# Attention in a language-model tower: the two heads of a pair in turns, both divided before one output projection, all sums of probabilities on GpSimd

## The reference, cut to what matters

```python
h = tok_table[x] + bias                                   # x: (2, 2048) tokens, 256 wide
def attn(x):                                              # x = layernorm(h)
    xn = layernorm(x) * norm_g + norm_b
    q = heads(xn @ Wq); k, v = split(x @ Wkv)             # 16 heads of 64
    k, v = concat(null_k, k), concat(null_v, v)           # 2 null keys: 2050 keys
    q, k = l2norm(q) * q_scale, l2norm(k) * k_scale
    sim = 8 * q @ k.T - slope[head] * abs(j - i)          # causal
    return merge(softmax(sim) @ v) @ Wout
h = h + attn(layernorm(h))
h = h + moe(layernorm(h))                                 # 8 experts of 256, top 2, and a shared one
```

## Time and profile before

| | |
|---|---|
| runs shown | 3328.92 us median of 3 (3328.67 to 3331.39) |
| profiled execution, its own time | 3325.87 us |
| its span, first to last instruction | 3323.9 us |
| PE, PEld, DVE, ACT, POOL busy | 90%, 44%, 61%, 45%, 49% |
| mean granted clock of PE | 0.962 of full speed |
| chain that ended last, shares | PE 63%, DVE 15%, POOL 11%, issue 9%, ACT 2% |

### The profile page before, as it was taken

The page is one execution under the profiler, slowest core; times in us unless marked ns, Lnnn a source line. Parts: engine busy times, 40 slices in busy tenths (PEclk is TensorE's granted clock), DMA queues, the critical chain, the costliest instruction groups (busy, mean ns, idle before and its releaser), DMA issues.

```text
span 3323.9 us, 50152 instructions
## 1 busy us (share of the span) xinstructions
PE 2989.6 (90%) x14241; PEld 1454.6 (44%) x14241; DVE 2013.1 (61%) x5648; ACT 1490.9 (45%) x2988; POOL 1631.9 (49%) x2152
## 2 busy tenths in 40 slices
PE   3589898989898987898989898989898989999999
PEld 2333434343434343434443434343434344666666
DVE  6666675666566658575757575756566663444444
ACT  3344555555555554555555555555555543111111
POOL 6454656565676564556565656565656543000000
PEclk9799999999999998999999999999999999999999
DMA  1000000000010000000000000000000100000000
GB/s 41 14 14 9 14 9 15 8 17 6 18 30 18 5 18 4 11 12 12 11 12 11 12 11 14 10 15 8 17 6 12 51 13 1 1 1 19 7 0 26
DMA packets 97495, 44.27 MB, mean 13 GB/s; under 512 B 38224, under 2 KB 96208, under 8 KB 97232
## 3 DMA queue, kind: packets, MB, share of 16 engines
q1 hardware_dynamic: 95696, 36.88, 4.3%
q0 software_dynamic: 1536, 4.20, 0.4%
HBM read 19.65 MB, written 4.19 MB: 7 GB/s over the span
## 4 chain that ended last, share of the span: by engine, by line
PE 63%; DVE 15%; POOL 11%; issue 9%; ACT 2%; DMA 0%; SPq 0%; DVEq 0%; POOLq 0%; ACTq 0%
PE ps L1146 13%; PE ps L1191 7%; PE ps L1204 7%; DVE ps L880 6%; PE ps L1130 5%; PE ps L1075 5%; PE ps L1163 5%; PE ps L1103 5%; PE ps L1131 4%; PE ps L1072 4%; PE ps L1153 3%; POOL rnorm L592 2%; POOL acc L628 2%; POOL tab_l L606 2%; DVE acc L915 1%
## 5 line engine op out<-in xcount | busy, mean ns | idle before, releaser
L715 ACT ACTIVATE probs<-ps,btab 128x512 f32<-128x512 f32 (+4 forms) x1408 | 768.3, 591 | 625.2 <-PE ps L1131 331.4
L628 POOL TENSOR_TENSOR acc<-acc,probs 128x512 f32<-128x512 f32 (+4 forms) x896 | 860.1, 960 | 162.6 <-ACT probs L715 84.3
L1146 PE MATMUL ps<-probs,arena 128*64 128x512 f32 (+4 forms) x2816 | 742.3, 530 | 0.0
L880 DVE CUSTOM_DVE_ANT_0 ps<-ps,tab_l 128x512 f32<-128x512 f32 (+1 forms) x896 | 568.2, 676 | 283.6 <-PE ps L1103 283.2
L1130 PE MATMUL ps<-arena 128*128 128x512 f16 (+4 forms) x1408 | 476.8, 339 | 0.7 <-issue 0.6
L1131 PE MATMUL ps<-arena 65*128 65x512 f16 (+9 forms) x1408 | 470.7, 336 | 0.0
L1163 PE MATMUL ps<-wo,otf 128*128 128x256 f32 (+1 forms) x1024 | 358.3, 432 | 5.6 <-DVE h L931 4.6
L931 DVE SCALAR_TENSOR_TENSOR h<-ps,rl,h 128x256 f32<-128x256 f32 x512 | 245.1, 479 | 132.0 <-PE ps L1163 131.5
L1103 PE MATMUL ps<-arena 64*128 64x512 f16 (+4 forms) x1408 | 256.7, 344 | 74.4 <-DVE mx L880 67.0
L592 POOL TENSOR_TENSOR rnorm<-nsq,minus_half 128x4 f32<-128x4 f32 (+1 forms) x272 | 298.3, 1097 | 22.7
L1072 PE MATMUL ps<-wqkv,xnT 128*128 128x128 f32 x1024 | 183.3, 304 | 136.0 <-DVE h L931 110.8
(11 more groups left out here) (128 smaller groups left out, 3753.7 us busy)
## 6 DMA issues: line engine op xcount, KB each, us to landing
arena<-arena SPq DMA_DIRECT2D x512, 32.0 KB, 1.9
wqkv<-in_Wkv SPq DMA_DIRECT2D x32, 128.0 KB, 2.4
wo<-in_Wout SPq DMA_DIRECT2D x64, 64.0 KB, 2.2
arena<-in_w SPq DMA_DIRECT2D x2, 2048.0 KB, 10.4
out<-h SPq DMA_DIRECT2D x8, 512.0 KB, 2.9
wqkv<-in_Wq SPq DMA_DIRECT2D x16, 128.0 KB, 2.4
arena<-augs SPq DMA_DIRECT2D x128, 1.0 KB
l_col<-arena SPq DMA_DIRECT2D x128, 2.0 KB, 2.0
```

The costliest lines, as they stand in the source:

```text
L628: pool.tensor_tensor(a, a, probs[0:rows, n % PB, 0:GW - c0], ALU.add).then_inc(sum_pool, 1)
L715: nc.scalar.activation(probs[0:rows, n % PB, 0:w], bank(S0 + n % 2)[0:rows, 0:w], ACT.Exp, bias=btab[0:rows, hh, z:z + 1]).then_inc(exp_do ...
L880: nc.vector.tensor_tensor_reduce(bank(A0 + hd)[:, 0:w], bank(A0 + hd)[:, 0:w], tab, 1.0, NEG, ALU.add, ALU.max, mx[:, hd, it, c:c + 1]).th ...
L1146: mm(bank(O0 + o % 2)[DH * z:DH * z + DH, c0:GW], vt[t % 2][0:rows, jt, hd, :], probs[0:rows, n % PB, 0:GW - c0], start=(jt <= (1 if ig el ...
```

## The change

The order and the work of the attention part change together:

- The blocks of the two heads come in turns (`block_of`): block m is head m % 2 of block m // 2. Head 0 writes rows 0 to 63 of the output bank and head 1 rows 64 to 127, in all groups.
- `sums` makes two matmuls with 64 output rows each, one per head, so that one bank holds the sums of both heads, each repeated over the rows of its head. A new DVE step, `divide`, takes the reciprocal of this 128x512 bank and multiplies the output bank by it. `wout` then is 4 matmuls per group for both heads, and `add_o` a plain addition. `keep_o`, `keep_l`, `turn_l` and `inv_l` go; Wout is held once, in one DMA per pair.
- `sum_p`: POOL adds up all groups (`DVE_SUMS` is empty). In groups 1 to 3 the first block isn't copied: the second block's addition reads both from `probs`. `acc` has 3 buffers instead of 2.
- `raw` goes: ACT copies q and k straight into `tqk`. `unit` is one multiplication for q and one per head for k, which takes the scale in as well; `scale_k` on POOL goes.
- `tables` moves from POOL to ACT; DVE adds the mask to `tab_r` before the first unit of a pair. The tables of pair t are planned at 88t-38, its projection from 88t-70 with a step of 5, its maxima from 88t-34.
- The start: fewer and later POOL steps for constants (`parameters` is separate), the zeros of the second arena later, shorter offsets between the steps of `embed` and `project`; the plan starts at -35 instead of -57, and the maxima of pair 0 are tied to the projections that they need. `embed` of the second sequence is spread with a step of 10 instead of 3.8 and ends in pair 7.

```diff
+    def block_of(m):
+        return (m % 2, *blocks[m // 2])
-    def side(m):
-        return m % 2 if blocks[m % BLKS][0] else 0
-    DVE_SUMS = (2,)
+    AB = 3
+    DVE_SUMS = ()
...
     def project(t, t0, step):
-            at(s0 + 2.9, "unit", t, s)
-            at(s0 + 3.0, "scale_k", t, s)
+            at(s0 + 2.6, "unit", t, s)
...
+        for ig in range(NG):
+            e0 = t0 + 2 * last_block[ig] + 1
+            at(e0 + 2.6, "sums", t, ig)
+            at(e0 + 3.2, "divide", t, ig)
+            for k in range(G):
+                w0 = max(e0 + 5.3, wout_from[0] + 2)
+                wout_from[0] = w0
+                at(w0, "wout", t, ig, k)
+                at(w0 + 0.6, "add_o", t, ig, k)
...
-    embed(0, -51, 2.2)
+    embed(0, -31, 2.6)
-    project(0, -44, 1.6)
-    maxima(0, -17, 0.9)
+    project(0, -24, 1.6)
+    maxima(0, -14.4, 1.1, lambda g: -24 + 1.6 * (2 * g + 1) + 8)
     for t in range(1, PAIRS):
-        project(t, PAIR * (t - 1) + 1.6, 3.2)
-        at(PAIR * t - 66.5 if t > 1 else 27, "tables", t)
-        if t > 1:
-            maxima(t, PAIR * t - 59.5, 1.85)
-        else:
-            maxima(t, 32, 1.75)
+        project(t, PAIR * t - 70, 5.0)
+        maxima(t, PAIR * t - 34, 1.85)
     for t in range(PAIRS):
+        at(PAIR * t - 38 if t else -16, "tables", t)
         attend(t, PAIR * t)
-        embed(b, PAIR * (b * NP - 2) + 50, 3.8)
+        embed(b, PAIR * (b * NP - 1) - 62, 10)
...
             def sum_p(t, m):
+                if on_dve or (ig > 0 and jt == 0):
                     return
+                if jt == (1 if ig else 0):
+                    need(pool, l_ready, (i - AB) // 2 + 1)
+                if ig == 0 and jt == 0:
+                    pool.tensor_copy(a, p).then_inc(sum_pool, 1)
                 else:
+                    first = ig > 0 and jt == 1
+                    pool.tensor_tensor(a, probs[0:rows, (n - 2) % PB, 0:GW] if first else a, p, ALU.add).then_inc(sum_pool, 1)
...
+            def tables(t):
+                need(act, a_read, 2 * UNITS * t)
+                need(act, aug_ready, NG * t)
+                for hd in range(2):
+                    nc.scalar.activation(tab_l[:, hd, :], pos[:, 0:512], ACT.Copy, scale=slope).then_inc(tab_ready, 1)
+                    nc.scalar.activation(tab_r[:, hd, :], pos[:, :], ACT.Identity, bias=back[:, hh:hh + 1], scale=slope).then_inc(tab_ready, 1)
+                    nc.scalar.activation(tab_k[:, hd, :, :], key0[:, :, :], ACT.Copy, scale=slope).then_inc(tab_ready, 1)
+                    nc.scalar.activation(tab_g[:, hd, :], group_pos[:, :], ACT.Copy, scale=slope).then_inc(tab_ready, 1)
...
             def unit(t, s):
+                if s < T:
+                    nc.vector.tensor_tensor(q, q, rnorm[0:rows, s % 2, 0:2].unsqueeze(2).to_broadcast([rows, 2, DH]), ALU.mult)
+                for hd in range(2):
+                    last = nc.vector.scalar_tensor_tensor(out=k[:, hd, :], in0=k[:, hd, :], scalar=rnorm[0:rows, s % 2, 2 + hd:3 + hd],
+                                                          in1=scl[0:rows, :], op0=ALU.mult, op1=ALU.mult)
...
+            def divide(t, ig):
+                o = NG * t + ig
+                dve.wait_ge(l_ready, o + 1)
+                nc.vector.reciprocal(rl[:, :], shared_of("sums", t, ig)[:, :]).then_inc(rl_ready, 1)
+                dve.wait_ge(rl_ready, o + 1)
+                dve.wait_ge(pv_done, PAIR * t + 2 * last_block[ig] + 2)
+                need(dve, w_ready, G * (o - 1))
+                nc.vector.tensor_tensor(otf[:, o % 2, :], bank(O0 + o % 2), rl[:, :], ALU.mult).then_inc(o_read, 1)
...
-                z = side(m)
-                mm(bank(O0 + o % 2)[DH * z:DH * z + DH, c0:GW], vt[t % 2][0:rows, jt, hd, :], probs[0:rows, n % PB, 0:GW - c0],
-                   start=(jt <= (1 if ig else 0)), stop=(jt >= G * ig + G - (1 if ig else 0))).then_inc(pv_done, 1)
+                mm(bank(O0 + o % 2)[DH * hd:DH * hd + DH, c0:GW], vt[t % 2][0:rows, jt, hd, :], probs[0:rows, n % PB, 0:GW - c0],
+                   start=(jt == 0), stop=(jt == G * ig + G)).then_inc(pv_done, 1)
...
+            def sums(t, ig):
+                for hd in range(2):
+                    last = mm(bank(z)[DH * hd:DH * hd + DH, :], ones[:, :], acc[:, (2 * (NG * t + ig) + hd) % AB, :], start=True, stop=True)
+            def wout(t, ig, k):
+                mm(bank(z)[:, 0:D], otf[:, o % 2, 128 * k:128 * k + 128], wo[:, r, :], start=True, stop=True).then_inc(w_ready, 1)
```

More of the change, by code:

```diff
@@ L923, in add_o @@
-            def add_o(t, hd, ig, k):
-                o = (2 * t + hd) * NG + ig
-                n = o * G + k
+                if jt == (1 if ig else 0):
+                    need(dve, l_ready, (i - AB) // 2 + 1)
+                if ig == 0 and jt == 0:
+                    nc.vector.tensor_copy(a, p).then_inc(sum_dve, 1)
+                else:
+                    first = ig > 0 and jt == 1
+                    nc.vector.tensor_tensor(a, probs[0:rows, (n - 2) % PB, 0:GW] if first else a, p, ALU.add).then_inc(sum_dve, 1)
@@ L1112, in scores @@
             def scores(t, m):
[L1113 removed]
+                hd, ig, jt, rows, c0 = block_of(m)
                 n, w = PAIR * t + m, GW - c0
```

295 lines of the change are left out of this document (120 added, 175 removed).

## The result

The changed kernel takes 3483.57 us (median of 4 runs, 3477.64 to 3484.27) against 3328.8 for the kernel before (4 runs, 3325.28 to 3331.39). The ratio is 1.0462, 95% interval 1.0444 to 1.048: 4.6% slower, where 9.6% faster was forecast. The profiled execution took 3477.64 us, its span is 3475.2.

What follows compares the result with a forecast made beforehand. PE was taken as the bound, with gaps mainly behind POOL's tables. Start -32, pair 0 -35, steady pairs -210, pair 6 -17 and pair 15 -25 sum to -319 from 3325.9: 3007, predicted 3010 us, range 2850 to 3140.

Steps and rivals of the forecast that it cites:

- The PE work: Steady pair: fewer or paired matmuls in `wout`, `sums` and group 0 of `values` save 17.5 us of 151.
- The reciprocal: New DVE division step: a reciprocal of 512 columns takes 3.4 us, or 4.3 by the skill's estimate.
- The stall behind it: PE waits after each division, in `scores_a` or `wout`: 2.2 us four times a pair, 8.8 us, ends 0 and 16.
- The tables on ACT: Eight table activations moved to ACT cost a steady pair 2 us, between 0 and 5.5.
- The gap behind POOL's tables: Projection wait for `add_o`, 7.9 us a pair, plus 1.4 of slow clock, goes when tables leave POOL: 9.3 us.
- DVE and POOL otherwise: Remaining load in a steady pair: DVE ends near 104 us, POOL at 102, costing PE 1 us.
- blocked `unit`: DVE's unit norm held up by POOL's SBUF use beyond the range; shares a 0.03 chance with a dearer reciprocal.
- POOL's jostling: POOL close to PE's pace in the wide blocks of a steady pair: 1 us a pair, ends 0 and 17.
- Rival 3: Slower kernel: POOL's waits per inverse norm push a steady pair over 171 us, whole up to 3500 us; chance 0.03.
- PE waits mostly for exponentials that wait for POOL: Stated sign of being wrong: POOL sets the pace in wide blocks, 3250 us, 3130 at half price; chance 0.22.
- Rivals 1: Division is covered, so a steady pair is PE-bound at 136.7 us and the whole takes 2840 us; chance 0.25.
- Rival 4: Two heads' matmuls don't overlap: two full blocks take 1.72 us, not 1.08; 18 us a pair, 3280 us; chance 0.02.

Runs made afterwards that it cites:

- The best version: Changed kernel with later unit norm, now on ACT, key scale on POOL, division in four, tables spread, projections 2 places earlier: 3027.4 us, ratio 0.9093.
- the single instruction: Changed kernel with the key scale left out, so the unit norm is one DVE multiplication instead of three narrow instructions: 3314.37 us.
- the improved one: Changed kernel with later unit norm, division in four parts and tables spread on ACT: 3141.36 us; with projections 2 places earlier 3064.83 us.

## Why the prediction was wrong

**The PE work** (17.5 us a pair off 151): right. The best version has 395.48 / 3 = 131.8 us of it at nearly the clock of before, where 133.5 was forecast. In the changed kernel it shows as 141, at a clock of 0.91: matmuls behind a gap run slower, as L1053 above. Apart from the 1.4 us behind the tables the sum had no term for that, and it is 7.5 of the 25.6 us by which a pair is over the forecast.

**The reciprocal**: right. 3.36 us for 64 of them, against 3.4; the 4.3 us, an estimate from the Trainium skill (VectorE: DVE Perf Modes, First, the fixed hardware budget), did not come. **The stall behind it**: right in place and about right in size. 8.8 us a pair was taken; cutting the division in four gave back 167 us, 10.4 for each of 16 pairs, but only 85 us, 5.3 a pair, once the unit norm was late. PE waits behind it for the output and then for the maxima, as forecast.

**The tables on ACT**: 2 us a pair was taken, the lump costs PE about 3.2 us (3.17 at 2008.20 in the changed kernel). Spreading them gave only 13.5 us in all.

**The gap behind POOL's tables, 7.9 + 1.4 us a pair**: here the prediction read the chain one step too far. It saw DVE stand still for an inverse norm queued behind the tables, and concluded that the gap goes when the tables leave POOL. But the fault was DVE's unit norm standing in front of `add_o` and the maxima, and whatever POOL has in front of the inverse norm takes the tables' place. The later unit norm in the kernel before shows it: tables left alone, PE's wait of 110.8 us falls to 5.6 and the time by 95 us.

**"DVE and POOL otherwise"** is the step that failed. POOL's busy time was right (102 us a pair, as forecast), DVE's was not (119 us, forecast 104). The step asked whether POOL is late for PE (1 us a pair for the jostling) and gave `unit` "0.3 more: 5 us" of busy time on a DVE with 40% to spare. It never asked what DVE does while POOL is late. Two things it left at nothing (a "blocked `unit`" beyond the range stands only among the chances, with a part of 0.03):

- *The wait.* POOL adds both heads in all groups, and the inverse norm stands behind up to seven of these additions. DVE waits up to 4.6 us, with the maxima behind it. The run with the later unit norm took most of the waits away and left most of the length: 16.9 us a steady pair.
- *The length.* Two more two-operand instructions came into `unit`, and all three grow while POOL adds: 2.1 us a projection instead of 0.70, 24 us of DVE time a pair instead of 5. The prediction weighed the Trainium skill's rule (SBUF — State Buffer, Who interferes with whom), worked out 10 us a pair by it and said "I count none of it". The trace agrees with the rule: 0.606 us for a 128x64 instruction beside full additions, 0.278 beside narrow ones. At the old place the length counts (169 us for the single instruction, 84.5 us in the kernel before); behind the later place alone hardly (17 us when it leaves DVE for ACT, net of what ACT then waits), and again once the division is cut (61 us).

The two can't be added: they are one lateness of DVE, which PE sees as waits for the maxima and for the shifts made from them. With POOL's additions shortened to 2 columns 352 us go, and a steady pair takes 153.7 us, 20.4 less than in the changed kernel and 5 above the forecast's 148.5; those 5 no run divides further. So the term "POOL's jostling, 1 us, ends 0 and 17" should have been some 21 a pair, above its upper end, by another route than the one considered.

**By stage** the miss of 470 us (3475.2 against a forecast span of 3005) lies in pairs 1 to 14 (2494.6 us, 407 more than forecast, the embedding's included), pair 15 (157.4 against 120) and pair 0 (186.3 against 155); the start was right (first exponential at 105.5 against 110), and the experts are untouched.

**The rivals.** Rival 3, the slower one, had the place half right (POOL's queue and its inverse norms) but the wrong victim: it priced POOL waiting for sums of squares and PE then waiting for exponentials. POOL does wait for them, 646.8 us in all, and PE's wait for exponentials is 65.9 us. "PE waits mostly for exponentials that wait for POOL" is therefore not how it went wrong, and that its 3500 us lies near the measured 3484 is luck. Rivals 1 and 4 did not occur: PE does wait behind the division, and two full blocks of `values` take 1.08 us, also in the changed kernel. Rival 4 was priced too low: its 1.72 us is by the prediction's own reading a block of 512 columns and one of 386, while two full ones would be nearer 2 x 1.04, the time of one such matmul alone.

**What stays open**: why 2 places in the start of the projections are worth 173 us in the changed kernel and 77 in the improved one. In the changed kernel neither the waits for inverse norms nor the lengths change much with them, in the improved one only the multiplication of q gets shorter. The edits that move work in the plan, the later unit norm among them, carry such an effect of the place as well. The rest of the new plan (the two heads in turns, the step of 5 places between projections, the place of the maxima) was never undone by itself, so what it adds to the loss isn't known.

## What to carry to other kernels

When an engine takes on work in an in-order queue, ask of each result that it hands to another in-order engine what is now in front of it, and what stands behind the instruction that waits for it there. An instruction that waits for a slow partner belongs late in its own queue, behind the work that the bottleneck needs: that took a few numbers in the plan and was worth 95 us in the kernel before and 244 in the changed one. A long instruction on an engine with 36% to spare still costs what it holds up; cut it so that urgent work fits between.

## What the runs showed of the hardware

DVE instructions on two SBUF operands grew by what POOL did beside them, more than by their size. In the changed kernel those of the unit norm for k took, as min/median/max in ns:

```profile
L827 DVE SCALAR_TENSOR_TENSOR tqk<-tqk,rnorm,scl x544: 263/276/1298, 50.0 to 2818.2; 128x64 f32<-128x64 f32 x171, 2x64 f32<-2x64 f32 x11
```

So about half of them were hardly held up, and the mean of 606 (in the three steady pairs) comes from the others. Where POOL's additions had 2 columns they took 262 to 283. POOL's own additions did not grow: 1.29 us for 128x512 in the changed kernel, 1.28 before. The reciprocal costs about 6.27 ns a column ((3356 - 172) / 508; the long one reads PSUM, the short one SBUF). A reciprocal of 128 columns in place in SBUF took 0.94 us in the split division, near the 0.953 of the earlier trace rows. ACT scaled 128x64 from SBUF by a column in 0.34 us with POOL adding beside it.
